# First layer's sums of a graph network on one Trainium2 core: the low halves move to GpSimd, all seven bins are weighed by VectorE and added as float32r pairs

## The reference

```python
hij = concatenate([h[src], h[dst]], axis=-1)
e = matmul(leaky_relu(matmul(hij, w), 0.2), a)
exp_e = exp(e)
denom = segment_sum(exp_e, src)
att = exp_e / denom[src]
out = segment_sum(h[src] * att, dst)      # the part that the change touches
x = layernorm(x + out)
```

## Time and profile before

| what | us |
|---|---|
| median of 3 runs (lowest, highest) | 3258.22 (3257.95, 3259.9) |
| profiled execution, first to last instruction (its span; the page gives no other time of it) | 3274.5 |
| busy in it: TensorE, VectorE, ScalarE, GpSimd | 3060.7, 3045.9, 2750.1, 155.0 |

### The profile page before, as it was taken

The page is one execution under the profiler, slowest core; times in us unless marked ns, Lnnn a source line. Parts: engine busy times, 40 slices in busy tenths (PEclk is TensorE's granted clock), DMA queues, the critical chain, the costliest instruction groups (busy, mean ns, idle before and its releaser), DMA issues. The chain is left out here.

```text
span 3274.5 us, 101508 instructions
## 1 busy us (share of the span) xinstructions
PE 3060.7 (93%) x40072; PEld 2792.8 (85%) x40072; DVE 3045.9 (93%) x4921; ACT 2750.1 (84%) x6946; POOL 155.0 (5%) x249
## 2 busy tenths in 40 slices
PE   5777699999999999699999999989999999999996
PEld 4666677778777877699999999988999999999994
DVE  8999889999999997799999999989999999999997
ACT  6988888888888885799999999987888888888887
POOL 0000000000000000000000000000111111111110
PEclk9989899999999997799999999999999999999998
DMA  3000022222222222234333333334455545554541
GB/s 66 13 14 11 23 98 93 87 93 94 93 87 93 94 86 48 65 96 97 97 97 96 97 96 97 97 93 137 161 163 160 164 161 163 161 163 161 162 151 41
DMA packets 173823, 333.06 MB, mean 102 GB/s; under 512 B 54876, under 2 KB 109616, under 8 KB 173264
## 3 DMA queue, kind: packets, MB, share of 16 engines
q1 hardware_dynamic: 170996, 323.30, 32.5%
q10 hardware_dynamic: 2348, 3.20, 0.4%
HBM read 320.77 MB, written 5.66 MB: 100 GB/s over the span
## 5 line engine op out<-in xcount | busy, mean ns | idle before, releaser
L1009 PE MATMUL l_gathered<-xp,l_src_onehot 128*128 128x128 bf16 x7203 | 467.0, 221 | 11.2 <-DVE l_src_onehot L922 11.2
L1436 PE MATMUL l_gathered<-hp,l_onehot 128*128 128x128 bf16 x7203 | 458.5, 219 | 0.0
L704 PE MATMUL sc_z<-sc_onehot,pq 128*128 128x256 f32 (+1 forms) x2450 | 429.4, 298 | 23.3 <-DVE sc_leaky L617 18.3
L1009 PEld LDWEIGHTS l_gathered<-xp,l_src_onehot 128*128 128x128 bf16 x7203 | 407.9, 99 | 26.3 <-DVE l_src_onehot L922 11.7
L788 ACT ACTIVATE sc_leaky<-sc_z 128x1024 f32<-128x1024 f32 (+3 forms) x325 | 309.8, 953 | 143.3 <-PE sc_z L708 140.5
L617 DVE SCALAR_TENSOR_TENSOR sc_leaky<-sc_z,sc_leaky 128x1024 f32<-128x1024 f32 (+3 forms) x325 | 370.1, 1139 | 60.0 <-ACT sc_leaky L788 52.5
L847 DVE TENSOR_TENSOR l_lane<-iota_b,l_lane_pairs 128x896 bf16<-128x896 bf16 x686 | 421.0, 614 | 0.0
L1436 PEld LDWEIGHTS l_gathered<-hp,l_onehot 128*128 128x128 bf16 x7203 | 406.1, 98 | 0.4
L708 PE MATMUL sc_z<-sc_onehot,pq 128*128 128x256 f32 (+1 forms) x2450 | 400.9, 286 | 0.0
L1450 PE MATMUL l_acc<-e,l_lane_wide 128*128 128x132 f32 x2744 | 385.5, 283 | 0.3 <-ACT e L1514 0.3
L704 PEld LDWEIGHTS sc_z<-sc_onehot,pq 128*128 128x128 f32 x2450 | 344.6, 196 | 35.9 <-issue 34.5
(11 more groups left out here) (246 smaller groups left out, 6107.4 us busy)
## 6 DMA issues: line engine op xcount, KB each, us to landing
rows_got<-edge_rows_wide SPq DMA_DIRECT2D x338, 448.0 KB, 3.7
l_got<-edge_rows_src SPq DMA_DIRECT2D x343, 224.0 KB, 3.2
placed<-edge_rows SPq DMA_DIRECT2D x144, 512.0 KB, 3.7
out_dram<-X SPq DMA_DIRECT2D x12, 256.0 KB
S<-edge_rows_wide SPq DMA_DIRECT2D x5, 448.0 KB, 8.4
edge_rows<-e SPq DMA_DIRECT2D x98, 6.1 KB
edge_rows_wide<-e SPq DMA_DIRECT2D x98, 12.2 KB
sc_last_rows<-edge_rows SPq DMA_DIRECT2D x24, 64.0 KB, 3.5
```

The costliest lines, as they stand in the source:

```text
L704: nc.tensor.matmul(z[:, b, 0:nw, :], PQ[:, b0 + b, q, 0:C], hot[:, r % HOTS, b, 0, 0:nw, :], start=(b == u and q == 0), stop=False)
L1009: ins = nc.tensor.matmul(gps[:, t % 2, i * P:(i + 1) * P], hot[:, t % RING, i, :], parts[:, g * GX + i, q, :], start=(q == 0), stop=(q == 2))
L1436: ins = nc.tensor.matmul(gps[:, t % 2, i * P:(i + 1) * P], dst_hot[:, t % RING, i, :], hp[:, g * GX + i, q, 0:C], start=(q == 0), stop=(q ...
```

## The change

All of it is in `layer0_sums`.

1. **weigh** on VectorE takes all seven bins (128x896); `weigh_late` on ScalarE is gone.
2. **take_high** on ScalarE takes all seven (128x896).
3. **take_low** moves from VectorE to GpSimd and takes all seven (128x896). GpSimd's `add_input` stands between its `take_low`s in program order.
4. **add_up** adds all seven bins as float32r pairs (7 matmuls of 256 columns; before 3 in float32 and 4 in float32r).
5. **Order and buffers.** TensorE gathers two rounds ahead (gather(t+2) before add_up(t)), the one-hot ring has 4 buffers, the loads 5, `msg` and `halves` 3 (`KEPT`). weigh(t) waits for take_low(t-3), take_high(t) for add_up(t-3). VectorE makes t+3 and finds the lanes of t, not of t+1; take, measure and average stand one round later.

```diff
-    RING, LOADS, SPLIT = 3, 4, 4
+    RING, LOADS, KEPT = 4, 5, 3
...
-        msg, halves = sb("messages", [P, 2, GX, C]), sb("message_halves", [P, 2, SPLIT, 2, C], F32R)
+        msg, halves = sb("messages", [P, KEPT, GX, C]), sb("message_halves", [P, KEPT, GX, 2, C], F32R)
...
                 def weigh(t):
                     n, g = divmod(t, PER)
                     dve.wait_ge(s["gathered"], t + 1)
-                    if t >= 2:
-                        dve.wait_ge(s["low"], t - 1)
-                    nc.vector.tensor_tensor(msg[:, t % 2, 0:SPLIT], gps[:, t % 2, 0:SPLIT * P].rearrange("p (i c) -> p i c", i=SPLIT),
-                                            e0[:, n, g * GX:g * GX + SPLIT].unsqueeze(2).to_broadcast([P, SPLIT, C]), ALU.mult
+                    if t >= KEPT:
+                        dve.wait_ge(s["low"], t - KEPT + 1)
+                    nc.vector.tensor_tensor(msg[:, t % KEPT], gps[:, t % 2, 0:GX * P].rearrange("p (i c) -> p i c", i=GX),
+                                            e0[:, n, g * GX:(g + 1) * GX].unsqueeze(2).to_broadcast([P, GX, C]), ALU.mult
                                             ).then_inc(s["messages"], 1)
-
-                def take_low(t):
-                    dve.wait_ge(s["high"], t + 1)
-                    nc.vector.tensor_tensor(halves[:, t % 2, :, 1, :], msg[:, t % 2, 0:SPLIT], halves[:, t % 2, :, 0, :], ALU.subtract
-                                            ).then_inc(s["low"], 1)
...
-                for t in range(-2, R):
-                    c = t + 3
+                for t in range(-3, R):
+                    c = t + 4
...
-                    if t + 2 < R:
-                        make(t + 2)
+                    if t + 3 < R:
+                        make(t + 3)
                     if t >= 0:
                         weigh(t)
-                    if 0 <= t + 1 < R:
-                        find_lanes(t + 1)
-                    if t >= 0:
-                        take_low(t)
-                    if t >= PER and t % PER == 2:
+                        find_lanes(t)
+                    if t >= PER and t % PER == 3:
                         take(t // PER - 1)
...
             @block.gpsimd
             def _(pool):
-                for n in range(NB):
+                def take_low(t):
+                    pool.wait_ge(s["high"], t + 1)
+                    nc.gpsimd.tensor_tensor(halves[:, t % KEPT, :, 1, :], msg[:, t % KEPT], halves[:, t % KEPT, :, 0, :], ALU.subtract
+                                            ).then_inc(s["low"], 1)
+
+                def add_input(n):
                     pool.wait_ge(s["taken"], n + 1)
                     nc.gpsimd.tensor_tensor(X[:, n, :], X[:, n, :], S[:, n, :], ALU.add).then_inc(s["summed"], 1)
+
+                for t in range(R):
+                    take_low(t)
+                    if t >= PER and t % PER == 3:
+                        add_input(t // PER - 1)
+                add_input(NB - 1)
...
                 def add_up(t):
                     n, g = divmod(t, PER)
-                    pe.wait_ge(s["late_messages"], t + 1)
                     pe.wait_ge(s["lane_wide"], t + 1)
                     if g == 0 and n >= 2:
                         pe.wait_ge(s["taken"], n - 1)
-                    for i in range(SPLIT, GX):
-                        nc.tensor.matmul(acc[:, n % 2, 0:C], lane_wide[:, t % 2, i, :].bitcast(F32), msg[:, t % 2, i, :],
-                                         start=(g == 0 and i == SPLIT), stop=False, skip_group_check=True)
                     pe.wait_ge(s["low"], t + 1)
-                    for i in range(SPLIT):
-                        last = g == PER - 1 and i == SPLIT - 1
+                    for i in range(GX):
                         ins = nc.tensor.matmul(acc[:, n % 2, 0:2 * C], lane_wide[:, t % 2, i, :],
-                                               halves[:, t % 2, i].rearrange("p h c -> p (h c)"), start=False, stop=last,
-                                               skip_group_check=True)
+                                               halves[:, t % KEPT, i].rearrange("p h c -> p (h c)"), start=(g == 0 and i == 0),
+                                               stop=(g == PER - 1 and i == GX - 1))
...
-                for t in range(-1, R):
-                    if t + 1 < R:
-                        gather(t + 1)
+                for t in range(-2, R):
+                    if t + 2 < R:
+                        gather(t + 2)
...
                 def take_high(t):
                     act.wait_ge(s["messages"], t + 1)
-                    nc.scalar.copy(halves[:, t % 2, :, 0, :], msg[:, t % 2, 0:SPLIT]).then_inc(s["high"], 1)
+                    if t >= KEPT:
+                        act.wait_ge(s["added"], t - KEPT + 1)
+                    nc.scalar.copy(halves[:, t % KEPT, :, 0, :], msg[:, t % KEPT]).then_inc(s["high"], 1)
```

More of the change, by code:

```diff
@@ L866, in layer0_sums @@
             "chain", "scaled", "scaled_late", "part_high", "part_rest", "part_middle", "part_low",
-            "hot", "staged", "lane", "lane_wide", "gathered", "messages", "late_messages", "high", "low", "added", "taken", "summed", "stats")}
+            "hot", "staged", "lane", "lane_wide", "gathered", "messages", "high", "low", "added", "taken", "summed", "stats")}
         loaded = [ctx.semaphore(f"l0_loaded{h}") for h in range(LOADS)]
@@ L972, in _ @@
                         part_low(c - 1)
-                    if t + 2 < R:
-                        make(t + 2)
+                    if t + 3 < R:
+                        make(t + 3)
                     if t >= 0:
                         weigh(t)
-                    if 0 <= t + 1 < R:
-                        find_lanes(t + 1)
-                    if t >= 0:
-                        take_low(t)
-                    if t >= PER and t % PER == 2:
+                        find_lanes(t)
+                    if t >= PER and t % PER == 3:
                         take(t // PER - 1)
-                    if t >= PER and t % PER == 4:
+                    if t >= PER and t % PER == 5:
                         measure(t // PER - 1)
-                    if t >= PER and t % PER == 5:
+                    if t >= PER and t % PER == 6:
                         average(t // PER - 1)
@@ L1005, in gather @@
                         pe.wait_ge(s["messages"], t - 1)
-                        pe.wait_ge(s["late_messages"], t - 1)
                     for i in range(GX):
@@ L1055, in widen @@
                     nc.scalar.copy(lane_wide[:, t % 2], lane[:, t % 2]).then_inc(s["lane_wide"], 1)
-                def weigh_late(t):
-                    n, g = divmod(t, PER)
-                    act.wait_ge(s["gathered"], t + 1)
-                    if t >= 2:
-                        act.wait_ge(s["added"], t - 1)
-                    for i in range(SPLIT, GX):
-                        b = g * GX + i
-                        ins = nc.scalar.activation(msg[:, t % 2, i, :], gps[:, t % 2, i * P:(i + 1) * P], ACT.Copy,
-                                                   scale=e0[:, n, b:b + 1])
-                    ins.then_inc(s["late_messages"], 1)
                 def take_high(t):
                     act.wait_ge(s["messages"], t + 1)
-                    nc.scalar.copy(halves[:, t % 2, :, 0, :], msg[:, t % 2, 0:SPLIT]).then_inc(s["high"], 1)
+                    if t >= KEPT:
+                        act.wait_ge(s["added"], t - KEPT + 1)
+                    nc.scalar.copy(halves[:, t % KEPT, :, 0, :], msg[:, t % KEPT]).then_inc(s["high"], 1)
                 def stage(n):
@@ L1085, in _ @@
                 part_middle(1)
-                widen(0)
+                part_high(3)
+                part_middle(2)
                 for t in range(R):
-                    c = t + 3
+                    c = t + 4
                     if c < PER:
@@ L1094, in _ @@
                         part_middle(c - 1)
-                    weigh_late(t)
                     take_high(t)
-                    if t + 1 < R:
-                        widen(t + 1)
+                    widen(t)
                     if t % PER == 3 and t // PER + 1 < NB:
```

## The result

The changed kernel takes 3571.5 us (median; 3571.0 to 3573.1), the kernel before 3258.2: a ratio of 1.095, 95% interval 1.0925 to 1.098, or 313 us slower. The forecast was 3612 us in a range of 3400 to 3770.

A forecast was written before the change was run, and what follows sets the result against it. GpSimd's take_low and VectorE's compare and make, excluding each other, were to bound the stage: 336 x (3.46 - 2.42) + 5 = +354 us, and 3258.2 + 354 = 3612 us, range 3400 to 3770. Before, three engines were level.

The forecast's parts named there:

- The bound and the four engines' work: Layer-0 stage, per round: TensorE 2.17 us and no longer the bound, ScalarE 1.88, VectorE 2.25, GpSimd's take_low 1.9.
- GpSimd's length: take_low of 896 columns on GpSimd: 1.9 us, from additions of 4 and 128 columns; bounds 0.32 and 2.24.
- The exclusion, both ways, for the whole instruction: GpSimd's take_low and VectorE's make and compare (find_lanes) cannot run together; 1.9 us holds VectorE to its end.
- E: Theory: GpSimd's subtraction and VectorE's compare and make exclude each other until over; the waiting one goes next; holds set the round.
- The turns: After VectorE's compare, GpSimd's waiting take_low goes first, 1.9 us, and make waits behind it.
- The round: Layer-0 stage: two rounds take 6.92 us, 3.46 us a round, from 2.42.
- The first seven: First rounds' two-input subtractions on VectorE, 1.08 us each, collide with take_low in a few of them: +5 us.
- VectorE keeps its turn: Rival: compare and make back to back, or the pair given up between rows; 2.9 to 3.2 us, 3420 to 3520; chance 0.16.
- The faster one: Rival: take_low holds the port under about 1.3 us and fits beside weigh; round 2.25 us, kernel 3201 us; chance 0.06.
- TensorE's lower clock: Part of the slower rival: TensorE idles, drops to 1.2 GHz; 4.2 us a round, 3856 us; chance 0.12 for both forms.

The follow-up runs named there:

- experiment 1: The changed kernel with the low halves of all seven bins back on VectorE, GpSimd keeping only its additions: 3449.6 us.
- experiment 4: The changed kernel with one added wait: GpSimd's take_low(t) also waits until VectorE has made the one-hots of round t+4: 3517.4 us.
- experiment 5: The changed kernel with GpSimd's subtraction cut into two or four instructions, all work done: 3384.3 us with two, 3477.2 with four.
- Experiment 3: The changed kernel with GpSimd taking low halves of only four, five or six bins, the others left zero: 3166.9, 3343.3 and 3481.7 us.
- experiment 7: The changed kernel with four, five, five bins as pairs, others full float32; VectorE takes none, one, two low halves: 3241.0, 3297.7, 3322.9 us.
- experiment 6: The changed kernel with GpSimd writing zeros by memset in place of the subtraction, low halves left out: 3130.1 us, run once.

## Why the prediction was right

**The bound and the four engines' work.** weigh 1.08 (measured 1.077), take_high 0.94 (0.939), the seven pairs 7 x 0.14 (0.90 from start to start, 0.08 less). Right. TensorE's share of the stage was to be 63% and is 74% (516 of 700 us): the 63% came from starts, while the profile adds up spans that overlap (1.34 + 1.05 = 2.39 us a round), part of them at a lower clock.

**GpSimd's length** was taken as 1.9 us from two points, with 2.24 as the upper end. Alone it spans 2.08, of which the port is held for 1.95 (from the compare's end at 1916.96 to 1918.91, in the timeline above). The Trainium skill's figure ("GPSIMD Engine Reference", section 3.1), by which I had estimated 1.97 us, came closest.

**The exclusion, both ways, for the whole instruction.** Right: the rows of operations of 0.3 us carried over to 2.1 us. Experiments 1, 4 and 5 do all the work of the change and alter who holds the port, how long at a time and in what order; the time changed each time in the way of E, by 122, 54 and 187 us (94 with four pieces), though experiment 4 and the cut in two missed E's size. Experiment 3 adds the length of the hold, with work left out. The exclusion for the whole instruction is also the rule of the Trainium skill, "SBUF — State Buffer", section "Who interferes with whom", and the trace agrees within 0.13 us (1.95 held of 2.08). Its further point, that a write-only GpSimd instruction leaves a two-input one of VectorE alone, no run here shows.

**The turns.** GpSimd gets in between compare and make, read from a single 4-column addition before: right (and a thin ground, one instance), and experiment 4 shows that this order costs 54 us.

**The round.** Forecast 3.46 us, measured 3.36: the term that was mis-sized, and the whole of the difference. The pair took 6.81 us, not 6.92: the two holds together 0.2 longer, compare and make behind a hold 0.48 and 0.25 instead of 0.54 and 0.36, and the hand-overs shorter by 0.2. Errors of either sign partly cancelled, which is luck. And not all rounds are paired: where add_input's addition takes GpSimd's turn, make waits for 0.2 us only, and two rounds of 2.2 and 3.0 us follow (weigh at 1902.41, 1904.64 and 1907.63). Sum: from the eighth weigh to the last 335 rounds of 3.352 us, 2.423 before, make 311 us. The first seven take 34.0 us, 32.5 before: 1.5 us, where I had put 5. That is 313, as measured.

**Rivals.** "VectorE keeps its turn" (2.9 to 3.2 us a round) is what the changed kernel would be with experiment 4's wait: 3.18. The faster one had its point right: with a hold below about 1.3 us the stage does gain, 91 us with four bins and three low halves left out, 0.6% with all work done (experiment 7). With seven bins the hold is 1.95, and that decided against it. TensorE's lower clock played no part: PEclk is 0.93 in the stage, and in a stretch at 0.85 (columns of the earlier trace rows) seven rounds take the same 23.51 us as the seven before them at 0.93:

```profile
1526.36:1549.87 23.51, 18.62 (x197) 17.37 (x197) 23.51 (x25) 13.03 (x15) 16.51 (x8) 0.85 0.22 69
```

## What to carry to other kernels

In this kernel GpSimd was no free engine beside VectorE's compare (two tiles of SBUF) and make (one bfloat16 tile of SBUF, 896 columns in 0.44 us). Look for GpSimd's few rows in the trace, see which VectorE spans end just behind them, and add the hold to the sum as if both were one engine. What lies under a VectorE instruction that isn't held, here weigh, which reads PSUM, costs nothing: up to a span of 1.28 us in experiment 3. But that rests on when GpSimd starts, not on the length alone: in experiment 7 spans of 1.28 and even 1.00 us held make for 0.5 to 1.1 us where take, measure or average stood ahead of it. So lay out the starts of every round, the rare instructions too; cut a longer GpSimd instruction in two, or leave the work where it was. Such a wait is found in no list of waits, only in spans longer than the instruction takes alone.

## What the runs showed of the hardware

- A subtraction of float32r from float32 on GpSimd, both tiles in SBUF: 1.00, 1.27, 1.54, 1.81 and 2.08 us for 384 to 896 columns, 2.1 ns a column, alone; VectorE does 896 in 1.07. A GpSimd memset of 896 float32 columns: 0.85 us.
- The wait for the port is counted as busy time of the waiting instruction, on both engines: VectorE's 96% in the changed kernel holds some 1.37 us a round of waiting.
- Taking work away or adding a wait can both turn the time by tens of microseconds, through whose turn it is: 54 us for one wait, 187 for one cut in two, 176 for one bin from four to five.
- Seven float32r matmuls of 256 columns follow each other at 0.13 us, a full float32 one of 128 columns takes 0.21: TensorE's share of the change was a gain of 0.3 us a round, from 2.39 to 2.06 or so (experiment 6), which only shows where GpSimd's hold is short.
